# Chunk sums in two fp32r passes, masked scores written in place, and another order at both ends of an adaLN block

## The chip, the cores and the metric

The kernel runs on one core of a Trainium2 chip, as one program. The metric is the device time of one execution in microseconds. The baseline is the median of three runs.

## What is computed

One adaLN-modulated block on x of 8 batches x 256 tokens x 128 channels, all in float32. A vector c of each batch gives six modulation rows of 128. The first half is a Mamba-2 style mixer, the second is a small transformer layer with a mixture of experts. Cut to what matters:

```
sa, ca, ga, sb, cb, gb = silu(c) @ wmod                     # ga, gb: sign(.) * max(|.|, 0.25)
h = layernorm(x) * (1 + ca) + sa
x = x + ga * mixer(h)
h = layernorm(x) * (1 + cb) + sb
x = x + gb * layer(h)

mixer: A = -exp(A_log) * softplus(h @ W_dt)                 # 4 heads
       conv over 4 taps of 384 channels, PReLU -> X (4 heads x 64), B (64), C (64)
       L[l, s] = exp(sum of A over s+1..l)  for s <= l      # the chunk sums
       Y = (C B^T * L) X  + carried state;  out = layernorm(gelu(h W2) * Y) W3
layer: rmsnorm, 16 heads of 8 with rotary embedding, causal softmax, Wo, residual,
       rmsnorm, router over 8 experts, best 2, silu(x Wg) * (x Wu) Wd with hidden 384, residual
```

## The kernel before, in words

The work is a sequence of three blocks, each with one program for every engine and barriers between them. Engines are ordered by semaphores alone.

**First block (pre).** SyncE loads PACK0 (c and wmod), PACK1, the four taps of the convolution weights CW, and PACK2. TensorE computes the modulation columns (L510), then *folds* the input projection into each tap (`fold`, three fp32 matmuls of 384 columns in bank 5 or 6, evicted to VH by ScalarE and split to VL by VectorE). `turned` transposes four normalised tiles. `modulate(b)` computes the modulation rows of batch b by one fp32 matmul of 512 columns (L535) in the same two banks, evicted by ScalarE to MB. `group` makes the dt and gelu projections of two batches (L527). The order on TensorE is written out: fold 0, fold 1, then transposes, two modulates and a group in turn, then modulates 4 to 7, fold 2, two groups, fold 3.

**Main block.** Eight batches go through stages A (convolution), B (mixer), C (attention) and D (router). `ORDER` gives for each engine one list of steps; a step with `-k` works in round r on batch r - k. Each engine runs its list round after round, in that order. PSUM banks are shared by fixed lists, and a bank is written again when its reader's semaphore says so. The steps of interest:

- `a_g(t)` on GpSimd (L1526): the product of a triangle TRI and the decays DA of one chunk, 128 x 512, into G (named DAT in the profile).
- `b_seg(t)` on TensorE (L837): the chunk sums, one fp32 matmul of the triangle UP with G; ScalarE takes the exponential into EL (L1072), GpSimd multiplies EL by CBS (L1536).
- `c_s(n)` on VectorE (L1385): for each group of heads, scores plus causal mask, reduced by max into MX. The elementwise result goes to JUNK in SBUF and is read by nobody. The negated maxima MN (L1396) are transposed (L938), copied to MT and sent by DMA into QT, for the second computation of the scores (`c_p`, L959), whose exponential ScalarE writes to PT.
- `signed` on VectorE (L1476 to L1483, tiles SIGN and MAG) treats the gates of MB in the first rounds.
- GpSimd also takes roots (RSB, RSX, RSR, RMD), sends rows to the experts' buffer (L289), and clears the masked half of PT (L1582). On the last batch ScalarE rounds the expert weights to EARLY_H, and VectorE (L1498) and GpSimd (L1590) subtract for EARLY_L.

**Expert block (moe).** 39 blocks of 128 rows in chunks of four. ScalarE's queue loads WD. TensorE counts rows (L1890), waits for WD and for the table of experts, warms up with ten fp32 matmuls of 512 columns (L1947), transposes the first block (`turn`, L1904), and then for each block runs gate and up (L1919), transposes the product (L1930) and multiplies by WD (L1939). ScalarE and VectorE split the transposed rows into XH and XL (`halves`). SyncE loads XB, one block at a time (L1721), when the sends have landed. GpSimd scatters results to rows_by_token (L1743). When all have landed, SyncE loads four YL tiles; VectorE adds the two experts' rows (L1877), multiplies by the gate (L1880), adds x (L1883), for four groups in turn; SyncE stores each.

## Time and profile before

| | us |
|---|---|
| three timed runs, median (lowest to highest) | 476.73 (475.59 to 480.74) |
| the profiled execution | 474.64 |
| its span, first to last instruction | 472.9 |
| busy: TensorE, VectorE, ScalarE, GpSimd | 383.0, 313.7, 242.4, 215.1 |
| mean granted TensorE clock | 0.875 |

The profile is of one execution. Start times count from the span's first instruction. A matmul in fp32 appears as two passes, one in fp32r as one; the ends of matmuls are modelled, so a busy TensorE isn't one at its peak. A line number is that of the listing above.

### The profile page before, as it was taken

The page shows a single profiled execution, that of the slowest core. Times are in us where ns is not written, and L with a number is a line of the kernel's source. Part 1 is how long each engine was busy: PE and PEld are TensorE (multiplying, and loading weights), DVE is VectorE, ACT ScalarE, POOL GpSimd, SP SyncE. Part 2 cuts the span into 40 slices and gives each one's busy share as a digit, 9 for nine tenths or more (in the row PEclk, how much of TensorE's full clock was granted, in tenths as well). Part 3 has the DMA queues.
Part 4 walks back from the last instruction along what each step waited for, and adds up shares of the span by engine and source line. Part 5 has one row for each costly group of instructions (what it writes and reads, how often), then busy time and mean ns, then how long its engine had stood idle before and what let it go on. Part 6 is the DMA issues. An engine that isn't in the chain of part 4 may idle for free. (4 is left out here: it accounts for less than half of the span.)

```text
span 472.9 us, 9431 instructions
## 1 busy us (share of the span) xinstructions
PE 383.0 (81%) x2798; PEld 296.5 (63%) x2798; DVE 313.7 (66%) x1255; ACT 242.4 (51%) x600; POOL 215.1 (45%) x253
## 2 busy tenths in 40 slices
PE   1796898697999999999898887856528899999940
PEld 1455777474768777777575654634313799999930
DVE  3523499987979899998969576478250455545416
ACT  1175643472767858587664737755210445545510
POOL 1111335443454774757564352656430169644430
PEclk9998799997999999999968696755658999999985
DMA  8300000000201102030120552002041112212116
GB/s 300 122 0 2 0 1 0 3 0 2 94 1 37 60 25 94 15 104 14 34 74 23 199 186 93 20 6 95 23 154 47 29 49 61 73 49 59 34 56 236
DMA packets 20993, 29.24 MB, mean 62 GB/s; under 512 B 2322, under 2 KB 17816, under 8 KB 20560
## 3 DMA queue, kind: packets, MB, share of 16 engines
q1 hardware_dynamic: 18240, 21.59, 13.9%
q0 software_dynamic: 2272, 4.43, 2.8%
q10 hardware_dynamic: 432, 2.62, 1.6%
q8 instruction: 24, 0.39, 0.4%
q14 instruction: 25, 0.20, 0.1%
HBM read 14.38 MB, written 14.25 MB: 61 GB/s over the span
## 5 line engine op out<-in xcount | busy, mean ns | idle before, releaser
L1385 DVE CUSTOM_DVE_ANT_0 JUNK<-bank,PACK 128x128 f32<-128x128 f32 (+1 forms) x256 | 74.2, 352 | 14.5 <-PE bank L927 14.5
L1743 POOL DMA_INDIRECT rows_by_token<-YB,IDX x39 | 38.1, 977 | 54.5 <-DVE YB L1849 50.1
L1169 ACT ACTIVATE PT<-bank 128x512 f32<-128x512 f32 x96 | 51.6, 617 | 17.3 <-PE bank L959 17.3
L1582 POOL TENSOR_SCALAR_AFFINE_SELECT PT<-PT 128x512 f32<-128x512 f32 x64 | 41.8, 671 | 20.1 <-ACT PT L1169 19.6
L289 POOL DMA_INDIRECT rows_by_expert<-XR,POS x32 | 32.0, 1001 | 16.5 <-POOLq L565 8.4
L800 PE MATMUL bank<-HTH,VH 128*128 128x256 f32 x96 | 31.9, 333 | 3.9 <-issue 3.9
L1863 DVE TENSOR_TENSOR GU<-bank,SG 128x384 f32<-128x384 f32 x39 | 21.7, 557 | 18.5 <-ACT SG L1788 14.5
L927 PE MATMUL bank<-KT,QT 32*128 32x128 f32 (+1 forms) x256 | 28.9, 327 | 5.4 <-DVE MX L1385 3.0
L1939 PE MATMUL bank<-WD,GUT 128*128 x234 | 32.6, 276 | 0.6 <-DVE YB L1849 0.6
L1919 PE MATMUL bank<-EARLY_H,XH 128*128 x78 | 29.6, 380 | 2.7 <-DVE XL L1832 2.1
L927 PEld LDWEIGHTS bank<-KT,QT 32*128 32x128 f32 x256 | 19.6, 201 | 19.1 <-DVE MX L1385 12.0
L1788 ACT ACTIVATE SG<-bank 128x384 f32<-128x384 f32 x39 | 19.2, 492 | 24.2 <-PE bank L1919 23.3
L959 PE MATMUL bank<-QT,KT 32*128 32x256 f32 (+1 forms) x256 | 24.8, 355 | 6.7 <-DMA QT<-MT 5.5
L1939 PEld LDWEIGHTS bank<-WD,GUT 128*128 128x128 f32 x234 | 29.2, 192 | 1.0 <-issue 1.0
L1570 POOL TENSOR_TENSOR QS<-TA,QS 128x256 fp32r<-128x256 f32 x16 | 11.9, 763 | 39.0 <-ACT QS L1134 39.0
L1536 POOL TENSOR_TENSOR EL<-EL,CBS 128x512 f32<-128x512 f32 x16 | 20.6, 1286 | 18.0 <-ACT EL L1072 11.7
L800 PE MATMUL bank<-HTL,VH 128*128 128x256 f32 x96 | 28.5, 297 | 0.0
L800 PE MATMUL bank<-HTH,VL 128*128 128x256 f32 x96 | 28.4, 296 | 0.0
L959 PEld LDWEIGHTS bank<-QT,KT 32*128 32x128 f32 x256 | 19.1, 234 | 12.9 <-DMA QT<-MT 5.9
L1849 DVE TENSOR_SCALAR YB<-bank,XB 128x128 f32<-128x128 f32 x39 | 13.7, 351 | 19.3 <-PE bank L1939 19.1
L1919 PE MATMUL bank<-EARLY_L,XH 128*128 x78 | 26.2, 336 | 0.0
L1919 PE MATMUL bank<-EARLY_H,XL 128*128 x78 | 26.2, 336 | 0.0
(246 smaller groups left out, 1047.6 us busy)
## 6 DMA issues: line engine op xcount, KB each, us to landing
rows_by_expert<-EMPTY SPq DMA_DIRECT2D x8, 1040.0 KB, 5.5
XB<-rows_by_expert SPq DMA_DIRECT2D x39, 65.0 KB, 1.8
CW<-in_convw SPq DMA_DIRECT2D x4, 576.0 KB, 10.6
YL<-rows_by_token SPq DMA_DIRECT2D x4, 512.0 KB, 5.2
RAW<-in_wg SPq DMA_DIRECT2D x1, 1536.0 KB, 7.0
RAW<-in_wu SPq DMA_DIRECT2D x1, 1536.0 KB, 11.7
WD<-in_wd ACTq DMA_DIRECT2D x1, 1536.0 KB, 7.2
X<-in_x ACTq DMA_DIRECT2D x2, 512.0 KB, 7.1
```

Source lines behind the costliest of these rows:

```text
L289: nc.gpsimd.indirect_dma_start(out=xs, out_offset=bass.IndirectOffsetOnAxis(ap=POS[p][:, n:n + 1], axis=0), in_=XR[p][:, n // 2, n % 2, :] ...
L800: last = pe.matmul(BANK[f"conv{c}"][:, 0:L], w, ht[:, steps_of(b, 1), k:k + L].rearrange("p b l -> p (b l)"), start=(k + m == 0), stop=(k ...
L927: last = pe.matmul(BANK[f"s{n}"][:, i * w:(i + 1) * w], QT[p][rows, g, t * 128:(t + 1) * 128], KT[p][rows, g, 0:w], start=True, stop=True)
L959: last = pe.matmul(BANK[f"p{n}"][:, i * w:(i + 1) * w], KT[p][rows, g, k], QT[p][rows, g, q], start=True, stop=True)
L1169: nc.scalar.activation(to, of, ACT.Exp, scale=AD ** -0.5).then_inc(p_ev.sem, 1)
L1385: last = nc.vector.tensor_tensor_reduce(out=JUNK[:, n % 2, i * w:(i + 1) * w], in0=BANK[f"s{n}"][:, i * w:(i + 1) * w], in1=MASK[:, 256 - ...
L1536: nc.gpsimd.tensor_tensor(EL[t][:], EL[t][:], CBS[:, t, :].unsqueeze(1).to_broadcast([128, NH, 128]), ALU.mult).then_inc(m_done.sem, 1)
L1582: nc.gpsimd.affine_select(out=block, in_=block, compare_op=ALU.is_ge, fill=0.0, base=0, pattern=[[0, NG], [1, 128]], channel_multiplier=-1 ...
L1743: nc.gpsimd.indirect_dma_start(out=yt, out_offset=bass.IndirectOffsetOnAxis(ap=IDX[c % NX][:, j:j + 1], axis=0), in_=YB[i % NYB][:], in_of ...
L1863: nc.vector.tensor_tensor(GU[i % 2][:], P[4 + i % 2][:, 0:HID], SG[i % 2][:], ALU.mult).then_inc(gu_done, 1)
L1919: last = pe.matmul(P[bank + i % 2][:, 0:HID], x[c % 2][:, at], w[n][:, bass.ds(e, 1), :].rearrange("p e h -> p (e h)"), start=(m == 0), st ...
L1939: last = pe.matmul(P[7][:, 0:D], GUT[i % 2][:, h * 128:(h + 1) * 128], WD[:, bass.ds(e, 1), h, :].rearrange("p e d -> p (e d)"), start=(h ...
```

## The change

It has five parts. The chunk sums are no longer one fp32 matmul but two fp32r matmuls into the same bank: the decays DA are split into a rounded part DAH and a remainder DAL, GpSimd forms a product with TRI for each, and TensorE accumulates both with a rounded copy of UP. The score reductions write their elementwise result over the scores in the bank instead of to JUNK, and no longer wait on the step before last; SIGN lies in O. In the first block, modulates 0 to 3 come before fold 0, modulates 4 to 7 take the places between the transposes and the groups, and fold 3 comes ahead of the last two groups. In the expert block, the warm-up has 8 matmuls and no longer waits for WD or the table; WD is waited for ahead of each down (it takes effect at the first), and two blocks are transposed before the first gate. At the end, YL 0 and 2 are loaded by SyncE and YL 1 and 3 by ScalarE's queue, group 1 is combined on GpSimd, and the stores go in the order 0, 2, 1, 3.

```diff
@@ pre, scalar @@
+                    for b in range(4):
+                        modulate(b)
                     fold(0)
                     fold(1)
...
-                    modulate(0)
-                    modulate(1)
+                    modulate(4)
+                    modulate(5)
                     group(0, 0)
-                    modulate(2)
-                    modulate(3)
+                    modulate(6)
+                    modulate(7)
                     group(1, 1)
-                    for b in range(4, B):
-                        modulate(b)
                     fold(2)
+                    fold(3)
                     group(2, 0)
                     group(3, 1)
-                    fold(3)
@@ pre, tensor @@
-                    pe.wait_ge(mod_col, 2)
-                    pe.wait_ge(in_pack[1], DMA)
...
                     def modulate(b):
-                        if b < 2:
-                            pe.wait_ge(v_lo, b + 1)
-                        else:
+                        if b in (4, 5):
+                            pe.wait_ge(v_lo, b - 3)
+                        elif b >= 2:
                             pe.wait_ge(mb_ev, b - 1)
...
                     def fold(k):
                         pe.wait_ge(in_conv[k], DMA)
+                        pe.wait_ge(mb_ev, k + 3 if k < 2 else B)
                         if k >= 2:
-                            pe.wait_ge(mb_ev, B)
                             pe.wait_ge(v_lo, k - 1)
...
+                    for b in range(4):
+                        modulate(b)
+                    pe.wait_ge(mod_col, 2)
+                    pe.wait_ge(in_pack[1], DMA)
                     fold(0)
                     fold(1)
                     turned(0, 0)
                     for g in range(NGRP - 2):
                         turned(g + 1, (g + 1) % 2)
-                        modulate(2 * g)
-                        modulate(2 * g + 1)
+                        modulate(4 + 2 * g)
+                        modulate(4 + 2 * g + 1)
                         group(g, g % 2)
                     turned(NGRP - 1, 1)
-                    for b in range(4, B):
-                        modulate(b)
                     fold(2)
+                    fold(3)
                     group(NGRP - 2, 0)
                     group(NGRP - 1, 1)
-                    fold(3)
@@ main @@
-                G = [ms(f"DAT{t}", [128, NH, 128]) for t in range(T)]
+                GH = [ms(f"DATH{t}", [128, NH, 128], R) for t in range(T)]
+                GL = [ms(f"DATL{t}", [128, NH, 128], R) for t in range(T)]
+                DAH, DAL = ms("DAH", [128, B * T, NH], R), ms("DAL", [128, B * T, NH], R)
+                UP_R = ms("UP_R", [128, 128], R)
...
-                JUNK = ms("JUNK", [128, 2, 4 * 128])
...
-                SIGN, MAG = ms("SIGN", [128, 2, D]), ms("MAG", [128, 2, D])
+                SIGN, MAG = O[:].rearrange("p t h d -> p t (h d)"), ms("MAG", [128, 2, D])
...
-                            pe.matmul(BANK[f"seg{t}"][:], UP, G[t][:].rearrange("p h l -> p (h l)"),
-                                      start=True, stop=True).then_inc(seg_ps.sem, 1)
+                            pe.matmul(BANK[f"seg{t}"][:], UP_R[:], GH[t][:].rearrange("p h l -> p (h l)"),
+                                      start=True, stop=False)
+                            pe.matmul(BANK[f"seg{t}"][:], UP_R[:], GL[t][:].rearrange("p h l -> p (h l)"),
+                                      start=False, stop=True).then_inc(seg_ps.sem, 1)
...
-                            need(dve, s_max.sem, s_max.at(b, n - 1))
                             apart(dve, parted)
                             for i, g in enumerate(gs):
                                 last = nc.vector.tensor_tensor_reduce(
-                                    out=JUNK[:, n % 2, i * w:(i + 1) * w],
+                                    out=BANK[f"s{n}"][:, i * w:(i + 1) * w],
...
+                        need(dve, dt_fix, 10)
+                        nc.vector.tensor_copy(UP_R[:], UP)
+                        nc.vector.tensor_copy(DAH[:], DA[:]).then_inc(da_split, 1)
+                        need(dve, da_split, 1)
+                        nc.vector.tensor_tensor(DAL[:], DA[:], DAH[:].bitcast(F), ALU.subtract).then_inc(da_split, 1)
...
-                                need(pool, dt_fix, 10)
+                                need(pool, da_split, 2)
                             need(pool, seg_ps.sem, seg_ps.at(b - 1, t + 1))
...
+                            for to, of in ((GH, DAH), (GL, DAL)):
+                                last = nc.gpsimd.tensor_tensor(
+                                    to[t][:], TRI.unsqueeze(1).to_broadcast([128, NH, 128]),
+                                    of[:, steps_of(b * 2 + t, 1), :].bitcast(F).rearrange("p t h -> p (t h)")
+                                    .unsqueeze(2).to_broadcast([128, NH, 128]), ALU.mult)
+                            last.then_inc(g_done.sem, 1)
@@ moe @@
-            NX, NYB, WARM_UP = 3, 4, 10
+            POOLS = 1
+            NX, NYB, WARM_UP = 3, 4, 8
...
-                return P[1 if part[0] == 1 else 0][:, 0:128]
+                return P[part[0] % 2][:, 0:128]
...
-                for g in range(B // 2):
+                for g in (0, 2):
                     sp.dma_start(YL[g][:], by_token[:, 4 * g:4 * g + 4]).then_inc(yl_in[g], DMA)
-                for g in range(B // 2):
+                for g in (0, 2, 1, 3):
                     sp.wait_ge(fin[g], 3)
...
+                need(pool, yl_in[POOLS], DMA)
...
+                nc.gpsimd.tensor_tensor(RES[POOLS][:], YL[POOLS][:, :, 0, :], YL[POOLS][:, :, 1, :], ALU.add
+                                        ).then_inc(fin[POOLS], 1)
...
                 halves(0, 0)
+                halves(0, 1)
                 for i in range(NBLK):
-                    if 0 <= i < CHK - 1:
+                    if 1 <= i < CHK - 1:
                         halves(0, i + 1)
...
+                for k in range(NYB):
+                    need(act, y_out[k], DMA * len(range(k, NBLK, NYB)))
+                for g in (1, 3):
+                    act.dma_start(YL[g][:], by_token[:, 4 * g:4 * g + 4]).then_inc(yl_in[g], DMA)
...
-                        need(pe, x_lo, 2)
+                        need(pe, x_lo, upto(0))
...
-                        need(pe, x_lo, 1 if n == 2 else 3)
+                        need(pe, x_lo, n - 1)
...
                 def down(i, e):
+                    need(pe, in_wd, DMA)
...
-                need(pe, in_wd, DMA)
-                need(pe, tbl_exp, 1)
                 for i in range(WARM_UP):
                     pe.matmul(P[2 + i % 2][:], IDENT, PACK[0][:, 0:512], start=True, stop=True)
+                need(pe, tbl_exp, 1)
                 turn(0, 0)
+                turn(0, 1)
...
-                    if i < CHK - 1:
-                        turn(0, i + 1)
+                    if i < CHK - 2:
+                        turn(0, i + 2)
```

## Rows read from the trace of the kernel before

**Rows 1.** Table by stretch: busy us and instructions of each engine, granted clock, DMA.

```profile
120.00:240.00 120.00, 115.61 (x1034) 86.15 (x1034) 108.76 (x506) 85.28 (x224) 70.73 (x90) 0.98 0.16 54
347.70:366.60 18.90, 10.94 (x24) 4.95 (x24) 4.45 (x17) 1.85 (x3) 3.93 (x4) 0.73 0.39 126
```

**Rows 2.** Timeline of VectorE, two rounds: start, length, then idle before, releaser.

```profile
164.28 0.29 DVE L1385 CUSTOM_DVE_ANT_0 JUNK<-bank,PACK 128x128 f32<-128x128 f32 x1 [0.40 <-PE bank L927]
...
192.60 0.29 DVE L1385 CUSTOM_DVE_ANT_0 JUNK<-bank,PACK 128x128 f32<-128x128 f32 x1 [0.40 <-PE bank L927]
```

**Rows 3.** Timeline of the first stage.

```profile
11.15 6.86 PE L544 MATMUL bank<-CW,PACK 128*128 128x384 f32 x12 [3.86 <-DMA CW<-in_convw]
...
17.85 0.60 PE L520 MATMUL bank<-PACK,XN 128*128 128x128 f32 x4
...
29.42 3.69 PE L535 MATMUL bank<-PACK,SIL 128*128 128x512 f32 x8
...
35.86 3.68 PE L527 MATMUL bank<-PACK,HG 128*128 128x260 f32 x16
...
39.38 2.10 PE L544 MATMUL bank<-CW,PACK 128*128 128x384 f32 x6
...
42.04 0.56 DVE L453 TENSOR_TENSOR VL<-bank,VH 128x384 fp32r<-128x384 f32 x1 [4.90 <-ACT VH L411]
```

**Rows 4.** Timeline of TensorE around a chunk sum; one row of the chain.

```profile
168.30 1.02 PE L837 MATMUL bank<-DAT,PACK 128*128 128x512 f32 x2
169.25 0.50 PE L927 MATMUL bank<-KT,QT 32*128 32x256 f32 x4
...
374.31 1.04 PE bank L1919 x6
```

**Rows 5.** GpSimd's products as a group; VectorE in the timeline.

```profile
L1526 POOL TENSOR_TENSOR DAT<-PACK,DA 128x512 f32<-128x512 f32 x16 | 17.3, 1082 | 15.2 <-DVE DA L1451 9.4 <-PE bank L837 5.6
...
74.89 1.50 DVE L1477 SCALAR_TENSOR_TENSOR MAG<-MB 128x256 f32<-128x256 f32 x1
...
65.05 0.42 DVE L1477 SCALAR_TENSOR_TENSOR MAG<-MB 128x256 f32<-128x256 f32 x1
...
173.91 0.88 DVE L187 TENSOR_SCALAR VED<-SSD 128x2 f32<-128x2 f32 x1
```

**Rows 6.** Groups of VectorE by form: busy us, mean ns, idle before, releaser.

```profile
L1385 DVE CUSTOM_DVE_ANT_0 JUNK<-bank,PACK 128x256 f32<-128x256 f32 x128 | 47.0, 419 | 4.9 <-PE bank L927 4.9
L1385 DVE CUSTOM_DVE_ANT_0 JUNK<-bank,PACK 128x128 f32<-128x128 f32 x128 | 27.7, 285 | 9.5 <-PE bank L927 9.5
...
L1303 DVE TENSOR_TENSOR GO<-bank,MB 128x256 f32<-128x256 f32 x8 | 3.3, 417 | 1.2 <-PE bank L879 1.1
L1359 DVE TENSOR_TENSOR TB<-QK,PACK 128x256 f32<-128x256 f32 x8 | 3.3, 417 | 0.0
```

**Rows 7.** Start of the experts: timeline, DMA issues, chain.

```profile
355.19 10.25 PE L1947 MATMUL bank<-PACK 128*128 128x512 f32 x20 [6.62 <-DMA WD<-in_wd]
356.79 13.02 SPq L1721 DMA_DIRECT2D XB<-rows_by_expert  x12
...
XB<-rows_by_expert SPq DMA_DIRECT2D x39, 65.0 KB, 1.8
...
373.20 0.44 PE bank L1904 x4
```

**Rows 8.** Tail and two streams at once: chain, timeline, a group.

```profile
458.22 3.84 DMA YL<-rows_by_token
...
462.15 0.69 DVE L1877 TENSOR_TENSOR RES<-YL 128x512 f32<-128x512 f32 x1 [7.09 <-DMA YL<-rows_by_token]
...
L1752 POOL TENSOR_TENSOR H<-H,MB 128x512 f32<-128x512 f32 x4 | 5.2, 1309 | 0.1
...
325.86 6.44 DVE L1498 TENSOR_TENSOR EARLY_L<-RAW,EARLY_H 128x384 fp32r<-128x384 f32 x8
325.87 3.75 POOL L1582 TENSOR_SCALAR_AFFINE_SELECT PT<-PT 128x512 f32<-128x512 f32 x4 [0.23 <-ACT PT L1169]
```

More of the change, by code:

```diff
@@ L1475, in signed @@
                             need(dve, mod_fix, n + 3 * i)
-                            nc.vector.tensor_scalar(SIGN[:], MB[:, now, m, :], 0.0, 2.0, ALU.is_ge, ALU.mult)
+                            nc.vector.tensor_scalar(SIGN, MB[:, now, m, :], 0.0, 2.0, ALU.is_ge, ALU.mult)
                             nc.vector.scalar_tensor_tensor(out=MAG[:], in0=MB[:, now, m, :], scalar=-1.0,
@@ L1482, in signed @@
                             need(dve, mod_fix, n + 3 * i + 2)
-                            nc.vector.scalar_tensor_tensor(out=MB[:, now, m, :], in0=SIGN[:], scalar=-1.0,
+                            nc.vector.scalar_tensor_tensor(out=MB[:, now, m, :], in0=SIGN, scalar=-1.0,
                                                            in1=MAG[:], op0=ALU.add, op1=ALU.mult
@@ L1758, in _ @@
                                                     ).then_inc(base, 1)
+                need(pool, yl_in[POOLS], DMA)
+                by_batch = RES[POOLS][:].rearrange("p (b t) d -> p b t d", t=T)
+                nc.gpsimd.tensor_tensor(RES[POOLS][:], YL[POOLS][:, :, 0, :], YL[POOLS][:, :, 1, :], ALU.add
+                                        ).then_inc(fin[POOLS], 1)
+                need(pool, fin[POOLS], 1)
+                nc.gpsimd.tensor_tensor(by_batch, by_batch, MB[:, steps_of(POOLS * 2, 2), GB, :].unsqueeze(2)
+                                        .to_broadcast([128, 2, T, D]), ALU.mult).then_inc(fin[POOLS], 1)
+                need(pool, fin[POOLS], 2)
+                nc.gpsimd.tensor_tensor(RES[POOLS][:], RES[POOLS][:], X[:, steps_of(POOLS * 4, 4), :], ALU.add
+                                        ).then_inc(fin[POOLS], 1)
             @block.scalar
@@ L1873, in _, with combined @@
                 need(dve, base, B)
[L1874 to L1884 removed]
+                def combined(g, n):
+                    by_batch = RES[g][:].rearrange("p (b t) d -> p b t d", t=T)
+                    if n == 0:
+                        need(dve, yl_in[g], DMA)
+                        nc.vector.tensor_tensor(RES[g][:], YL[g][:, :, 0, :], YL[g][:, :, 1, :], ALU.add
+                                                ).then_inc(fin[g], 1)
+                    elif n == 1:
+                        need(dve, fin[g], 1)
+                        nc.vector.tensor_tensor(by_batch, by_batch, MB[:, steps_of(g * 2, 2), GB, :].unsqueeze(2)
+                                                .to_broadcast([128, 2, T, D]), ALU.mult).then_inc(fin[g], 1)
+                    else:
+                        need(dve, fin[g], 2)
+                        nc.vector.tensor_tensor(RES[g][:], RES[g][:], X[:, steps_of(g * 4, 4), :], ALU.add
+                                                ).then_inc(fin[g], 1)
+                for g in range(B // 2):
+                    for n in range(3 if g != POOLS else 0):
+                        combined(g, n)
             @block.tensor
```

16 lines of the change are left out of this document (2 added, 14 removed).

## The prediction

> **What bounds the kernel now.** I read the page first, then the table by stage, then the two ends and one round of the middle in order of time. The page names TensorE and VectorE as the busiest, but the table by stage shows that no engine bounds all of it. I use five stages: the first (0 to 42.6 us), the main one (to 347.7), the start of the experts (to 366.6), the expert blocks (to 455) and the tail (to 472.9). In the middle of the main stage, 120 to 240 us, TensorE is busy 115.61 of 120 us and VectorE 108.76 [rows 1]: two engines run nearly full and hand a short wait to and fro. At the first scores of a round VectorE waits 0.40 us for TensorE, at 164.28 and again one round of 28.3 us later [rows 2]. That wait is what TensorE can give back in such a round; what it saves beyond that is not seen. At the start of the experts TensorE is busy 10.94 of 18.90 us [rows 1], most of it warm-up. The expert blocks are one unbroken chain of TensorE.
>
> The profiled execution took 474.64 us for a span of 472.9; the three timed runs have the median 476.73 (475.59 to 480.74). I sum against 474.64 and add 1.0 at the end, about half of what the profiled run lies under the median.
>
> **First stage.** It is a chain on TensorE [rows 3]. TensorE idles 3.86 us until the first CW has landed at 11.15, folds twice (L544), transposes from 17.85, and later runs eight modulate passes (L535) from 29.42. A fold follows, two groups (L527) from 35.86 for 3.68 us, the last fold from 39.38 for 2.10 us, and that fold's split on VectorE ends at 42.60, 1.1 us behind it. The change puts four modulates into the idle time before 11.15 (their operands come with the first pack), and the last fold ahead of the two groups. So from 29.42 there remain two folds and the groups: 29.4 + 2 x 2.1 + 3.7 = 37.3, and with 1.0 us for the evictions behind the last group 38.3 against 42.6: **-4.3 us**. The new waits of the folds ask for modulates' evictions that are finished by then. The first folds run at the low clock now, as their row shows: 12 passes in 6.86 us, where the last fold does 6 in 2.10 [rows 3]. TensorE begins its steady work some 3.8 us earlier after the change, and if the clock rises as long after that as now, the folds themselves run at the full rate and end up to 1.8 us before 17.85; if it doesn't, four modulates at the low rate (1.7 us each, from the eight passes in 3.69 at the full one) push the folds back and they end where they do now. I take the middle, **-0.8**. Together -5.1, ends -4 and -6.5.
>
> **Chunk sums.** Each sum was one fp32 matmul of 512 columns, two passes in the records, 0.95 us from its start at 168.30 to the next at 169.25 [rows 4], twice that at the half clock. The new pair of fp32r passes has no row of 512 columns. The nearest is L1919: six passes of 384 columns in 1.04 us [rows 4], 0.173 each, so 0.23 for 512 and 0.46 a pair. Sixteen sums save 16 x 0.49 = 7.8 us of TensorE, up to 9 with those at the half clock. Little of it lies on the path: in a steady round the first sum stands ahead of VectorE's wait of 0.40 us, the second ahead of VectorE work that is late anyway. Six such waits and 1 us for a sum at the half clock near 112 us give -3.4. Ends: 0 if VectorE's wait has another cause, -9 if all counts.
>
> GpSimd pays for it. Each operand was one product of 1.08 us, 17.3 us in 16 [rows 5]; now there are two, so +17 us. GpSimd is half idle and almost nobody waits for it, so the product as such is hidden. But a VectorE instruction that reads two SBUF operands, or a TENSOR_SCALAR in SBUF, stands still while a GpSimd instruction runs: MAG takes 1.50 us at 74.89 and 0.42 at 65.05, and VED, of two elements, 0.88 us at 173.91, beside a product [rows 5]. The score reductions read one operand from PSUM; with means of 419 and 285 ns they are not touched, and their 74.7 us in eight batches are a third of a round [rows 6]. So of 17 us two thirds meet VectorE work that can be stopped, and such work waits for half a product on average: 17 x 0.67 x 0.5 = **+5.6** (0 to +11, if each waits for all of it). Behind a round's second product GpSimd has RMD, RSR and an EL product, which come 1.05 us later, and ScalarE's XR and QK after them; in the two rounds where scatters fill GpSimd's queue that can cost 1 us more, which the upper end holds. The set-up adds three short VectorE instructions and a wait of GpSimd's first product on them (0.6 us); TensorE's first sum waits for a table load of ScalarE anyway, so nothing. Main stage: -3.4 + 5.6 = **+2.2**, ends -7 and +9.
>
> **Scores in place.** VectorE's 256 reductions write into the bank that they read and no longer to JUNK. Their own wait on the step before last goes; VectorE is idle ahead of them for TensorE alone (4.9 and 9.5 us, all for L927, [rows 6]), so it was free. No row here has VectorE write to PSUM. Lower bound: nothing, since reading from PSUM costs nothing either (GO from PSUM 417 ns, TB from SBUF 417 ns, both of 256 columns, [rows 6]). Upper bound: read and write of one bank exclude each other and each element counts twice; 128 more columns are 134 ns, so 128 x 0.134 + 128 x 0.268 = 51 us. I take 0, because the equal pair is nearest. Where JUNK and SIGN lie moves no instruction.
>
> The Trainium skill (VectorE: DVE Perf Modes, section on the TRN2 errata) gives a VectorE instruction 58 cycles of fixed cost from SBUF and 120 from PSUM. The equal pair above does not show that difference. Were the 62 cycles (65 ns at its 0.96 GHz) to come with a write to PSUM, the estimate would be 256 x 65 ns = 17 us of VectorE.
>
> **Start of the experts.** TensorE waits 6.62 us for WD, warms up for 10.25 us from 355.19 and only then turns the first block [rows 7]. The change warms up at once, with 8, and waits for WD only at the first down; WD lands at 355.2 and then has nothing behind it. Warming up from 348.6 takes 8.2 us at today's mean, 13.7 if all of it runs at the half clock; the end is 357 (362). Next in line is the load of the blocks: SyncE issues 12 of them in 13.02 us from 356.79, 1.085 apart, each landing 1.8 us later [rows 7], the first at 358.6. The first expert matmul then comes near 360.1. But the transposes of the second chunk need the eighth block: issue 364.4, landing 366.2 or a little later. They stand at 373.20 in the chain now [rows 7], and behind them all is as before and full. Gain: 373.2 - 366.6 = 6.6 us. TensorE idles some 2.5 us ahead of that landing, and a stretch of half clock behind it would cost 1.5 to 3. I take **-5.2** (-2.5 to -6.6).
>
> **Tail.** One queue loads four YL; the first lands 3.84 us after its issue, and VectorE runs 12 instructions of 0.69 us, 8.3 us in all [rows 8]. After the change YL0 and YL1 are issued side by side and share the DMA, so YL0 lands later. VectorE keeps nine, GpSimd takes three, of 1.3 us by the nearest row, L1752 of the same shape [rows 8]. Both read two SBUF operands. What two such streams cost together is seen at 325.86: eight VectorE subtractions of 384 columns take 6.44 us, 0.8 each and twice what their length asks, while four GpSimd selects take 3.75 [rows 8]: they take turns. So 9 x 0.69 + 3 x 1.3 = 10.1 us against 8.3, less 0.6 for overlap, is +1.2, and the later landing +0.6: **+1.8** (-1 to +3). The Trainium skill (SBUF — State Buffer, section Who interferes with whom) calls the pair of ports that the two engines share an exclusive lock; by that rule, the turns of 325.86 agree.
>
> Sum: -5.1 + 2.2 + 0 - 5.2 + 1.8 = -6.3; 474.64 - 6.3 + 1.0 = **469.3 us**, 1.6% under the median. A measurement of this kernel can tell about 1% from no change.
>
> **The rivals.** (a) Contention eats the gain, no change: the added products stop VectorE for most of their length (+10), the sums give -3.4, the tail +3, the ends -4.5 and -4.5. That is +0.6, **476 us**. For it: VED waited almost a whole product. Against: many products fall beside the reductions. (b) TensorE sets the rounds, and all it saves counts: -9 + 3 there, -6 and -6 at the ends, tail 0: -18, **458 us**. Against it stands VectorE with 108.76 us busy in 120. (c) Slower: the write into the bank just read lengthens each reduction. Some 160 of the 256 stand before 240 us, where VectorE has no slack, so the gain of 6.3 is gone from 6.3/160 = 39 ns an instruction on; at the upper bound of 51 us some 35 are exposed, **504 us**, at half of it 487. For it speaks only that no row shows such a write. (d) The reordering at the start of the experts buys nothing because the clock falls back: start -2.5, inside my range.
>
> **Chances.** Forecast (464.5 to 472) 0.53; (a), 472 to 478, 0.25; (b), 457 to 464.5, 0.12; (c), 478 and above, 0.10. The range, 462 to 477, leaves out (c) and the far parts of (a) and (b). Faster by over 1% is under 472.0: 0.53 + 0.12 = 0.65; (a) is the middle, 0.25; (c) is slower, 0.10.
>
> **What would show it.** The first stage ends near 38. The sums are two fp32r passes, 0.46 us a pair; GpSimd has 32 products; HN, MAG, MB, VED and VER grow in mean, and VectorE's busy time up to 240 us rises by 5 us. The reductions stay at 285 and 419 ns; if they grow, (c) is on. The first expert matmul comes 12.5 us after the stage begins, with a wait for XB ahead of the second chunk's transposes. In the tail VectorE's RES instructions grow from 0.69 to some 1.5 us while GpSimd's run. The prediction fails if a round of the main stage changes by more than 1 us either way.

## The result and the profile after

The changed kernel takes 489.54 us (489.43 to 492.46, three runs) against 476.73: the ratio is 1.027, 95% interval 1.0185 to 1.0355. It is slower, by 12.8 us where 7.4 less were forecast. The profiled execution has a span of 487.7 us against 472.9. Executions of one kernel here can lie 10 us apart and more, each with its own mean clock, so a small difference of two medians says little.

I put the same instruction of both traces side by side at the borders of the stages. The first stage ends 4.28 us earlier than before; the main stage is 23.1 us longer (its end stands 18.83 later); the start of the experts takes back 5.72; the expert blocks are equal; the tail costs 1.7. That is -4.3 + 23.1 - 5.7 + 1.7 = 14.8, the whole difference. So three of the four stages that were changed do what was forecast, and the loss is in the middle.

Table by stretch of the kernel after, columns as in [rows 1]: the steady part of the main stage, then a look at 170 to 190 us in steps of 4.

```profile
120.00:240.00 120.00, 112.59 (x970) 86.48 (x970) 102.46 (x455) 78.46 (x198) 70.25 (x89) 0.90 0.13 44
...
174.00:178.00 4.00, 4.00 (x29) 3.23 (x30) 3.97 (x13) 2.66 (x12) 3.59 (x4) 1.00 0.10 33
178.00:182.00 4.00, 2.46 (x16) 1.69 (x15) 3.93 (x17) 3.15 (x10) 2.08 (x3) 0.94 0.00 0
182.00:186.00 4.00, 4.00 (x15) 3.23 (x16) 3.68 (x16) 2.04 (x6) 1.32 (x2) 0.50 0.69 229
186.00:190.00 4.00, 4.00 (x22) 3.55 (x21) 1.27 (x3) 1.71 (x4) 0.09 (x1) 0.50 0.14 48
```

The granted clock from 120 to 240 us is 0.90 where it was 0.98 [rows 1]. TensorE is busy 2.46 of 4 us from 178, and behind that it works at the lower of its two levels, 1.2 GHz, for some 10 us (181.5 to 191.8 in a table by single microseconds). The kernel before has no such stretch there: its rows of 120 to 230 us are all at 1.00.

What VectorE does before that, in the groups by form (all of VectorE, to compare with [rows 6]) and in the timeline from 165 and from 175 us:

```profile
L1389 DVE CUSTOM_DVE_ANT_0 bank<-bank,PACK 128x256 f32<-128x256 f32 x128 | 50.8, 453 | 1.9 <-PE bank L932 1.8
L1389 DVE DVE_READ_ACCUMULATOR2_ANT MX<- 128x1 f32 x256 | 35.5, 139 | 0.0
L1389 DVE CUSTOM_DVE_ANT_0 bank<-bank,PACK 128x128 f32<-128x128 f32 x128 | 32.3, 326 | 14.1 <-PE bank L932 14.0
```

```profile
165.42 0.33 DVE L1389 CUSTOM_DVE_ANT_0 bank<-bank,PACK 128x128 f32<-128x128 f32 x1
165.67 0.14 DVE L1389 DVE_READ_ACCUMULATOR2_ANT MX<- 128x1 f32 x1
165.67 0.33 DVE L1389 CUSTOM_DVE_ANT_0 bank<-bank,PACK 128x128 f32<-128x128 f32 x1
...
175.26 1.06 POOL L1537 TENSOR_TENSOR DATH<-PACK,DAH 128x512 fp32r<-128x512 f32 x1
175.46 1.88 DVE L187 TENSOR_SCALAR VED<-SSD 128x2 f32<-128x2 f32 x1
176.25 1.05 POOL L1537 TENSOR_TENSOR DATL<-PACK,DAL 128x512 fp32r<-128x512 f32 x1
```

Two things are seen. The reductions grew from 285 to 326 and from 419 to 453 ns, and reading the accumulator from 82 to 139. They overlap, so the price is read from start to start: the median over 128 each is 0.249 us against 0.211 for 128 columns and 0.382 against 0.345 for 256. That is 38 ns for either length, a fixed cost. And VED, two elements long, took 1.88 us: it waited for both products, one after the other, where it took 0.88 beside one [rows 5]. This happens in two of the eight rounds, as before; in the other six VED takes 0.16 to 0.17 us.

The edges, in the timeline of the kernel after. The last two folds run as one block, and the groups end at 37.5; the warm-up starts by itself and the first expert matmul stands 13.35 us after the stage's begin; a sum is two passes.

```profile
29.95 4.04 PE L542 MATMUL bank<-CW,PACK 128*128 128x384 f32 x12
...
33.83 3.68 PE L525 MATMUL bank<-PACK,HG 128*128 128x260 f32 x16
...
377.86 0.30 PE L1942 MATMUL bank<-PACK,XB 128*128 128x128 f32 x1 [0.81 <-DMA XB<-rows_by_expert]
...
379.85 0.68 PE L1957 MATMUL bank<-EARLY_H,XH 128*128 x1 [0.73 <-ACT XH L1796]
```

```profile
476.08 0.69 DVE L1909 TENSOR_TENSOR RES<-YL 128x512 f32<-128x512 f32 x1 [7.91 <-DMA YL<-rows_by_token]
476.52 1.37 POOL L1775 TENSOR_TENSOR RES<-YL 128x512 f32<-128x512 f32 x1 [6.61 <-DMA YL<-rows_by_token]
476.81 1.63 DVE L1913 TENSOR_TENSOR RES<-RES,MB 128x512 f32<-128x512 f32 x1
...
484.59 0.69 DVE L1917 TENSOR_TENSOR RES<-RES,X 128x512 f32<-128x512 f32 x1
```

In the tail VectorE's instructions grow to 1.63 us while GpSimd's run, and the combine takes 9.2 us instead of 8.3.

### The profile page after: what moved, and what is told of

Read it like the earlier page. It is cut to its first block and busy times, and to the rows that moved or that the text cites. A ratio compares the mean times of both kernels' runs of the same rounds, so it can differ in the third digit from the quotient of the medians.

```text
span 487.7 us, 9446 instructions
## 1 busy us (share of the span) xinstructions
PE 399.6 (82%) x2794; PEld 314.0 (64%) x2794; DVE 329.3 (68%) x1255; ACT 244.0 (50%) x600; POOL 236.7 (49%) x272
## 5 line engine op out<-in xcount | busy, mean ns | idle before, releaser
L1389 DVE CUSTOM_DVE_ANT_0 bank<-bank,PACK 128x128 f32<-128x128 f32 (+1 forms) x256 | 82.5, 390 | 15.9 <-PE bank L932 15.8
L289 POOL DMA_INDIRECT rows_by_expert<-XR,POS x32 | 31.8, 993 | 16.5 <-POOLq L565 8.4
L1893 DVE TENSOR_TENSOR GU<-bank,SG 128x384 f32<-128x384 f32 x39 | 21.7, 557 | 22.2 <-ACT SG L1813 14.0
L932 PE MATMUL bank<-KT,QT 32*128 32x128 f32 (+1 forms) x256 | 29.7, 336 | 7.9 <-DVE MX L1389 4.3
L1389 DVE DVE_READ_ACCUMULATOR2_ANT MX<- 128x1 f32 x256 | 35.5, 139 | 0.0
L803 PE MATMUL bank<-HTH,VH 128*128 128x256 f32 x96 | 32.2, 335 | 3.7 <-issue 3.7
L1582 POOL TENSOR_TENSOR QS<-TA,QS 128x256 fp32r<-128x256 f32 x16 | 11.9, 764 | 41.1 <-ACT QS L1139 41.1
L964 PE MATMUL bank<-QT,KT 32*128 32x256 f32 (+1 forms) x256 | 26.3, 371 | 5.7 <-DMA QT<-MT 4.6
L803 PE MATMUL bank<-HTH,VL 128*128 128x256 f32 x96 | 30.3, 316 | 0.0
L803 PE MATMUL bank<-HTL,VH 128*128 128x256 f32 x96 | 30.2, 314 | 0.0
L1978 PEld LDWEIGHTS bank<-WD,GUT 128*128 128x128 f32 x234 | 29.2, 192 | 1.0 <-issue 1.0
L964 PEld LDWEIGHTS bank<-QT,KT 32*128 32x128 f32 x256 | 20.5, 249 | 10.6 <-DMA QT<-MT 4.8
L981 PE MATMUL bank<-PT,V 128*32 128x256 f32 x256 | 26.0, 475 | 1.6 <-POOL PT L1594 1.4
## 6 DMA issues: line engine op xcount, KB each, us to landing
RAW<-in_wu SPq DMA_DIRECT2D x1, 1536.0 KB, 11.9
```

Of the source, the lines that this page charges most:

```text
L289: nc.gpsimd.indirect_dma_start(out=xs, out_offset=bass.IndirectOffsetOnAxis(ap=POS[p][:, n:n + 1], axis=0), in_=XR[p][:, n // 2, n % 2, :] ...
L803: last = pe.matmul(BANK[f"conv{c}"][:, 0:L], w, ht[:, steps_of(b, 1), k:k + L].rearrange("p b l -> p (b l)"), start=(k + m == 0), stop=(k ...
L932: last = pe.matmul(BANK[f"s{n}"][:, i * w:(i + 1) * w], QT[p][rows, g, t * 128:(t + 1) * 128], KT[p][rows, g, 0:w], start=True, stop=True)
L964: last = pe.matmul(BANK[f"p{n}"][:, i * w:(i + 1) * w], KT[p][rows, g, k], QT[p][rows, g, q], start=True, stop=True)
L981: pe.matmul(o[:, at:at + L], V9[p][:, 0, h, :], PT[:, j, g, 0:L], start=True, stop=False, tile_position=(0, 32 * g))
L1389: last = nc.vector.tensor_tensor_reduce(out=BANK[f"s{n}"][:, i * w:(i + 1) * w], in0=BANK[f"s{n}"][:, i * w:(i + 1) * w], in1=MASK[:, 256 ...
```

## The experiments

Each is compared with the kernel before on the same chip. Medians are given with the lowest and highest time and, where there is one, the ratio with its 95% interval; the mechanism is read from the one profiled execution. Five chips were used (e1 to e4, e5 to e8, e9 to e12, e13 to e15, e16 and e17), on which the kernel before had medians of 476.1 to 479.7, so microseconds of different groups compare less well than ratios. All but e4 and e12 start from e1 or from e3.

| run | what it is | us, median (lowest to highest) | ratio to before |
|---|---|---|---|
| e1 | ends only | 467.88 (467.2 to 468.9) | 0.9835 (0.980 to 0.987) |
| e2 | + in place | 479.56 (473.5 to 481.6) | 1.003 (0.999 to 1.008) |
| e3 | + split sums | 476.80 (473.1 to 483.3) | 0.999 (0.994 to 1.003) |
| e4 | after, old tail | 488.73 (486.5 to 490.8) | 1.027 (1.021 to 1.032) |
| e5 | + second product alone | 483.03 (481.5 to 487.6) | 1.012 (1.003 to 1.021) |
| e6 | + fp32r sums, one product | 465.70 (462.7 to 480.3) | 0.9685 (0.961 to 0.976) |
| e7 | + 1.4 us of VectorE once | 470.26 (469.3 to 474.2) | 0.985 (0.977 to 0.993) |
| e8 | e3, VED and VER on GpSimd | 470.20 (469.9 to 470.4) | 0.982 (0.976 to 0.988) |
| e9 | e1, VED and VER on GpSimd | 475.36 (470.4 to 485.1) | 0.998 (0.992 to 1.004) |
| e10 | e9, old tail | 482.17 (471.4 to 487.4) | 1.0225 (1.011 to 1.034) |
| e11 | e3, product moved | 493.05 (487.8 to 495.3) | 1.043 (1.034 to 1.053) |
| e12 | after, VED and VER on GpSimd | 484.82 (483.3 to 489.5) | 1.023 (1.018 to 1.029) |
| e13 | e1, EL waits for MN | 471.82 (465.0 to 479.9) | none |
| e14 | e9, EL waits for MN | 474.01 (469.2 to 475.5) | 0.995 (0.991 to 1.000) |
| e15 | e11, product waits for MN | 475.96 (470.4 to 480.1) | none |
| e16 | e1 again | 469.23 (468.0 to 474.6) | 0.986 (0.980 to 0.992) |
| e17 | e1, old tail | 467.17 (465.2 to 474.1) | 0.978 (0.973 to 0.984) |

Where rounds are spoken of, this is the distance between the first BATCH_NORM_STATS2 on STATB of one batch and the next, for batches 0 to 7, in us:

| kernel | rounds |
|---|---|
| before | 17.7 15.8 25.8 29.1 28.3 27.9 27.7 |
| after | 18.7 18.8 26.1 29.8 34.2 31.4 29.8 |
| e1 | 17.7 17.0 26.2 29.1 28.3 27.9 27.3 |
| e2 | 17.7 17.1 26.4 29.8 29.0 29.2 31.0 |
| e3 | 18.7 18.6 25.8 28.9 32.1 31.2 28.1 |
| e7 | 17.7 16.7 27.0 29.1 32.7 27.7 26.6 |
| e8 | 18.7 18.6 25.7 28.6 28.5 29.1 28.7 |
| e9 | 17.6 17.0 26.1 29.2 31.8 28.3 27.7 |
| e10 | 17.6 16.8 27.0 29.1 28.9 29.7 30.1 |
| e11 | 18.7 17.8 27.5 33.2 34.5 32.4 29.4 |
| e12 | 18.7 18.6 26.0 29.5 32.5 32.2 30.4 |
| e15 | 18.7 18.0 27.7 29.8 28.5 28.5 27.5 |

**e1, e2, e3: the parts.** e1 undoes both edits of the main stage, with the wait on s_max and the one fp32 matmul; e2 and e3 undo one each:

```
-                                    out=BANK[f"s{n}"][:, i * w:(i + 1) * w],
+                                    out=JUNK[:, n % 2, i * w:(i + 1) * w],
...
-                            for to, of in ((GH, DAH), (GL, DAL)):
...
+                            nc.gpsimd.tensor_tensor(
+                                G[t][:], TRI.unsqueeze(1).to_broadcast([128, NH, 128]),
```

> The kernel after with its two edits of the main stage undone: the reductions write to JUNK again, and a chunk sum is one fp32 matmul over one GpSimd product. Left of the change: first stage, start of the experts, tail. Theory A (the loss comes from the two edits of the main stage, the rest works as predicted): the span shows -4.3 us at the end of the first stage, the main stage is as long as before (305 us within 3), the start of the experts gives -6, the tail +1.7, so 464 to 467 us. Theory B (the clock did it: the first stage starts the rounds at another phase of the clock, and the rounds lose by that alone): the main stage is 10 us or more longer than before though its instructions are the same, and the time is 476 or more.

> e1 and the reductions writing in place, into the bank that they read. The sums stay one fp32 matmul over one product. Theory A1 (the write to PSUM is the main cost): each reduction keeps the 38 ns more from start to start that the kernel after shows (0.249 against 0.211 us for 128 columns, 0.382 against 0.345 for 256), 256 of them 9.7 us of VectorE, most of it exposed and with more half clock behind it: 475 to 485 us. Theory A2 (GpSimd's second product is the main cost): 38 ns a reduction stay, but in the rounds where TensorE has slack or the clock is low they hide, at most 4 us over e1: under 471.

> e1 and the split chunk sums: two fp32r passes over two GpSimd products. The reductions write to JUNK as in the kernel before; for want of space JUNK is of two bytes an element here and shares its space with MAG. The start-to-start time of a reduction should be 0.211 and 0.345 us whatever the type; if it is not, the type of the output counts and the run says less. Theory A2 (GpSimd's second product holds VectorE up, VED above all, which took 1.88 us at 175.46 against 0.88 before, and TensorE then idles and loses its clock): VED stays near 1.9 us in these rounds and the time is 8 us or more over e1, 474 or more. Theory A1: sums save 0.49 us each and the products cost as much, within 3 us of e1: 463 to 469.

Theory A holds and B is out: e1's steady rounds are those of the kernel before to 0.1 us, and it is 1.65% faster than before (467.88 us, 0.9 over the range that I gave). In place alone costs 11.7 us over e1, the split alone 8.9, and both together (the kernel after) 21.7: nearly their sum. A1 and A2 were put as alternatives; both are true. In the profiled executions the main stage grows by 1.8 us in e1, 12.0 in e2, 11.9 in e3 and 23.1 in the kernel after. For the spread of one execution: e16, which has e1's instructions, shows 4.8 where e1 shows 1.8. e2 keeps the 38 ns (medians 0.249 and 0.382); e3 has 0.211 and 0.345 with its two-byte JUNK.

```profile
171.88 2.27 DVE L187 TENSOR_SCALAR VED<-SSD 128x2 f32<-128x2 f32 x1
172.08 1.05 POOL L1540 TENSOR_TENSOR DATH<-PACK,DAH 128x512 fp32r<-128x512 f32 x1
173.08 1.04 POOL L1540 TENSOR_TENSOR DATL<-PACK,DAL 128x512 fp32r<-128x512 f32 x1
```

```profile
174.00:178.00 4.00, 2.30 (x14) 1.32 (x12) 3.93 (x19) 2.41 (x8) 2.77 (x4) 1.00 0.00 0
...
182.00:186.00 4.00, 4.00 (x22) 3.55 (x21) 1.78 (x5) 2.07 (x4) 1.39 (x3) 0.50 0.34 113
```

These are e3's timeline and its table by stretch: VED stands until the second product ends, TensorE runs dry, and the clock falls. Nothing in e3's reductions changed but the type of JUNK.

What TensorE waited for from 120 to 240 us (total, times, longest), in e1 and then in e3:

```profile
PE bank L938 <- DVE MN L1399: 0.9, 2, 0.5
```

```profile
PE bank L945 <- DVE MN L1406: 2.1, 4, 0.7
PE bank L208 <- ACT XR L202: 2.1, 2, 1.0
```

So the late VED reaches TensorE on two ways. One is VectorE's own order: MN comes later. The other is longer: GpSimd takes the root RMD of VED, ScalarE makes XR with it, and TensorE's L208 needs XR. Of the 1.7 us that TensorE idles from 174 to 178 us, 1.00 is for XR and 0.70 for MN; in e1 it never waits for XR in these rounds.

**e4: the tail undone in the kernel after** (one queue, twelve instructions on VectorE).

> The kernel after with the tail undone: four loads of YL on SyncE's queue, all twelve instructions of the combine on VectorE, stores in order. All else as after. By the trace of after the tail grew by 1.7 us (from the last expert block to the end: 22.8 to 24.6 us), of it 1.0 while VectorE's instructions take 1.6 us beside GpSimd's. If that is the cause: 1.5 to 2 us less than the kernel after, 487.5 us, and each RES instruction at 0.69 us. If the later landing on two queues is nothing but a shift of the same bytes: less than 0.7.

0.8 us less, inside the spread and under the 1.5 to 2 expected; in the trace the tail is 1.8 us shorter, and each RES takes 0.69 us.

**e5, e6: the product and the sums apart.** e5 makes the one product of e1 twice (the added lines above the mark in the middle), e6 takes e3 and reads the high half twice, without the low product:

```
+                            for sem in (once, g_done.sem):
...
+                                if sem is once:
+                                    need(pool, once, 2 * b + t + 1)
...
-                            pe.matmul(BANK[f"seg{t}"][:], UP_R[:], GL[t][:].rearrange("p h l -> p (h l)"),
+                            pe.matmul(BANK[f"seg{t}"][:], UP_R[:], GH[t][:].rearrange("p h l -> p (h l)"),
```

> e1 (ends of the change alone, 467.88 us) with each GpSimd product made twice, the sums still one fp32 matmul: the added product without what it is for. Theory C (the loss of e3 is the product: two in a row hold VectorE's two-element VED for up to 2.3 us, TensorE runs out of work at the end of the round and its clock is halved): the time is 9 to 14 us over e1, 477 to 482, above e3's 476.8 by what the fp32r passes save; VED takes 1.9 us or more in the rounds from 171 and 202. Theory D (the loss of e3 comes from the fp32r sums themselves, say a TensorE with less work that loses its clock): within 2 us of e1.

> e3 with one product: both fp32r passes read the high half (the low half's product is left out, so the low part of each decay is missing from the sums and the high part counts twice). The saved TensorE time without GpSimd's second product. Theory C: the sums save 0.5 us each and nothing is held up longer than before, 1 to 4 us under e1, 464 to 467. Theory D: 4 us or more over e1, 472 or more.

The product alone costs 2.9% (1.012 against e1's 0.9835; 15 us by the medians). The sums alone gain 2.2 us by the medians and 1.5%, some 7 us, by the ratios, since the kernel before was slower beside e6 than beside e1 (479.7 against 477.8); between these it stays open. D is out. e6's profiled execution is its slowest (480.3, the other four 462.7 to 467.2), so no row of it is used. A point I had wrong is seen in e5:

```profile
175.73 0.88 DVE L187 TENSOR_SCALAR VED<-SSD 128x2 f32<-128x2 f32 x1
...
177.21 0.51 DVE L1347 TENSOR_SCALAR VER<-SS 128x2 f32<-128x2 f32 x1
...
179.01 1.26 POOL L1540 TENSOR_TENSOR EL<-EL,CBS 128x512 f32<-128x512 f32 x1
179.11 1.20 DVE L1397 TENSOR_SCALAR MN<-MX 128x32 fp32r<-128x32 f32 x1
```

Between its two products GpSimd waits on a semaphore, and VED slips in after one, 0.88 us, not the 1.9 expected. The loss is there all the same: everything behind the products on GpSimd is a microsecond late, so the EL product now starts just ahead of MN and holds it for all of its length. TensorE waits 0.6 us for XR and 0.6 for MN there.

**e7: one late VectorE step.**

```
+                        d_variance(dve, b)
+                        if b == 1:
+                            nc.vector.tensor_reduce(MAG[:, 0, 0:5], MASK[:].unsqueeze(1).to_broadcast([128, 5, 256]),
```

> e1 with one added VectorE instruction in one single round, behind VED of the second batch (at 169.5): the maximum of 5 x 256 columns of the mask, some 1.4 us, as long as VED was held more in e3 (2.27 against 0.88). Nothing else is changed and GpSimd does nothing more. Theory E (one late VectorE step of this size empties TensorE at the end of the round, and the chip then grants half the clock for some us): VectorE's next rounds stand 3 to 5 us later than in e1, with a stretch at half clock near 178 to 190 that e1 does not have; the whole run is 3 to 6 us over e1, if rounds further on lose by it too up to 9. Theory F (delays just add): 1.4 us, and TensorE's clock is as in e1 there.

```profile
171.21 1.48 DVE L1507 TENSOR_REDUCE MAG<-PACK 128x5 f32<-128x1280 f32 x1
```

```profile
174.00:178.00 4.00, 2.23 (x21) 2.22 (x21) 3.90 (x14) 2.97 (x8) 1.46 (x2) 1.00 0.01 4
178.00:182.00 4.00, 4.00 (x22) 3.20 (x20) 3.79 (x17) 1.42 (x5) 1.41 (x2) 0.58 0.81 270
182.00:186.00 4.00, 4.00 (x30) 3.75 (x30) 0.53 (x4) 2.78 (x6) 1.22 (x2) 0.56 0.01 2
```

Theory E for the round: one instruction that VectorE is 1.4 us later by makes that round 4.3 us longer (32.7 against 28.3), with half clock from 178.6 on. For the whole run it was too high: in the trace two thirds are given back later, where half clock falls in other places, and the median is 2.4 us over e1 and 1.0 over e16, which has e1's instructions. So a growth of the round is shown, and a loss of the whole run is not.

**e8, e9, e10, e12: VED and VER on GpSimd**, where their roots are taken (VER in the same way):

```
-            nc.vector.tensor_scalar(VED[:], SSD[:], 1.0 / D, RMS_EPS, ALU.mult, ALU.add
+            nc.gpsimd.tensor_scalar(VED[:], SSD[:], 1.0 / D, RMS_EPS, ALU.mult, ALU.add
```

> e3 (split sums, JUNK) with VED and VER computed by GpSimd, right ahead of the roots that take them, and no longer by VectorE. The two products stand where they stood. Theory C: no VectorE instruction of the round's end is held by the products, the clock stays up in 125 to 230 us as in e1, and the time is within 3 us of e1: 465 to 471. If the held VED is not the cause but GpSimd's later roots are (RMD and RSR come 1 us later than in e1, and ScalarE's XR and QK after them): the rounds stay as long as in e3, 474 to 479.

> e1 with VED and VER computed by GpSimd, as in e8, and one product a sum. In e1 VED waits 0.7 us for the product in two of the eight rounds, and the first MN 0.4 us for the EL product behind it. Theory C: VectorE gets these back in the rounds at full clock, but GpSimd's roots come 0.3 to 0.6 us later and QK behind them: 0 to 3 us under e1, 465 to 468. If the later roots cost more than the holds: over 469.

> e9 with the tail of the kernel before (one queue for the YL loads, the combine on VectorE alone). By e4 against the kernel after the change of the tail costs 0.8 us: 0.5 to 1.7 us under e9. If under 464, the fastest version so far.

> The kernel after with nothing else changed than VED and VER on GpSimd. In it both costs of the main stage act: the 38 ns more a reduction and the products. If the two costs are separate, this takes back what e8 took from e3 (6.6 us, from 489.5 to 481 to 485) and leaves e2's cost. If the reductions alone keep VectorE so late that TensorE loses its clock in any case: above 486.

e8 takes back 6.6 of e3's 8.9 us by the medians, and all of them by the ratios (0.982 against e1's 0.9835), with both products in place, and e3's two long rounds are gone (28.5 and 29.1). TensorE still waits 1.2 us for XR in such a round, but no longer for MN, and the clock from 172 to 202 us stays at 1.00. Its first two rounds are still 2.6 us longer than e1's together; by which instruction was not traced. e12 takes back 4.7 by the medians, inside the range expected of two separate costs, but this is weak: the ratios are 1.023 and 1.027 with intervals that overlap, and its profiled execution, the slowest, has long rounds (32.5 and 32.2) and a main stage as long as that of the kernel after (23.0 us over before). But e9, the same patch with one product, is a miss, 7.5 us over e1 by the medians, and 4.9 if in each kernel only the executions within 1.5% of its fastest are taken:

```profile
172.08 1.26 POOL L1530 TENSOR_TENSOR EL<-EL,CBS 128x512 f32<-128x512 f32 x1
172.23 1.15 DVE L1390 TENSOR_SCALAR MN<-MX 128x32 fp32r<-128x32 f32 x1
```

```profile
170.00:174.00 4.00, 3.00 (x19) 1.89 (x18) 3.21 (x12) 3.20 (x9) 3.03 (x5) 1.00 0.00 0
...
178.00:182.00 4.00, 4.00 (x22) 3.55 (x21) 2.18 (x5) 1.91 (x4) 1.41 (x3) 0.50 0.44 149
```

With VED gone VectorE comes to MN earlier and GpSimd to EL later, and MN is held 1.15 us, not 0.62 as in e1. MN is what TensorE waits for, 1.00 us here. e8 escapes it, for its EL starts after MN. Whether this is what e9 loses by is open. e10 has the same main stage, the same hold (1.16 us at 173.94) and the same wait of 1.00 us, and its clock stays at 1.00 from 122 to 202 us: that round takes 28.9 us, where e9's takes 31.8. And the traced execution of e9 is its fastest, with a main stage 4.8 us over before, as in e16. e10 is a miss as well: 0.5 to 1.7 us under e9 were expected, and its median is 6.8 over it, with executions 16 us apart; in its trace the tail alone is 1.8 us shorter, as it should be.

**e11, and the waits of e13 to e15.** e11 moves "Ag1" in GpSimd's order from ahead of RMD, RSR and EL to behind them. e13 to e15 add one wait, `need(pool, mn.sem, mn.at(..., 2))`, ahead of the second EL (e13, e14) or of the moved products (e15).

> e3 (split sums, JUNK) with the second chunk's two products moved in GpSimd's order from ahead of RMD, RSR and EL to behind them, where GpSimd waits 4.5 us for ScalarE. VED and VER stay on VectorE. Theory C: VED takes 0.2 to 0.4 us in all rounds; the products meet MN, XC and TA instead, which read SBUF twice or are held as VED was, and cost part of it back. 467 to 474. If it is not who is held but that there is a product at all (its traffic), the time stays as e3's, 475 to 478.

> e1 with one added wait: GpSimd's second EL product starts only when VectorE has written MN. In e1 the first MN takes 0.62 us at 172.50 beside that product, and TensorE waits 0.45 for it. Theory G (what counts is whether the step that TensorE waits for is held): MN 0.18 us in the rounds at full clock, TensorE's waits for MN go from 0.9 us to under 0.2 between 120 and 240 us, XC and TA are held instead without harm: 0 to 3 us under e1, 465 to 468. Theory H (the amount of contention counts, wherever it falls): no gain, 467 to 471.

> e9 (475.4; VED and VER on GpSimd) with the same added wait. Theory G: the first MN falls from 1.15 us to 0.18, TensorE's clock stays up from 125 to 215 us, and the time is 464 to 469, 6 us or more under e9. Theory H, or the later roots as the cause: as e9, 472 to 478.

> e11 (493.1; split sums, the second chunk's products behind EL) with the products waiting for MN. Theory G: both MN take 0.2 us instead of 0.9, TensorE's waits for MN go from 6.2 us to under 1.5 between 120 and 240, the rounds from 34 to 28.5 to 30, and the time is 467 to 476, 17 us or more under e11. Theory H: XC, TA and TB are held for the same 2 us, and the time stays over 485.

e11 is the slowest of all, though VED took 0.16 us. TensorE's waits from 120 to 240 us (total, times, longest) in e11 name the cause; in e15, under it, MN is down to 0.3 us, and these are the longest:

```profile
PE bank L945 <- DVE MN L1406: 6.2, 4, 1.7
```

```profile
PE bank L966 <- DVE HV L1259: 2.5, 4, 0.7
PE bank L895 <- DVE HX L1348: 1.0, 1, 1.0
...
PE bank L945 <- DVE MN L1406: 0.3, 1, 0.3
```

One wait, with the same instructions, brings e11 from 493.1 to 476.0 and its rounds from 34.5 to 28.5; the executions don't overlap (487.8 to 495.3, 470.4 to 480.1). That is theory G, and H, that contention costs the same wherever it falls, is out there. It mends what the move in e11 broke: against e3, 476.8 us, nothing is gained. And e13 and e14 say how far G goes; both came out where H had them, or above. Their MN are at 0.18 us and their steady clock up to 210 us is 1.00, and they gained nothing that can be told (e14 is 1.4 us under e9 by the medians, e13's executions span 15 us): XC and TA are held instead, and in e13 TensorE waits for PRIOR (0.7 us once) and POSB (0.5 once), which e1 does not show. So one more wait is worth it where TensorE stalls for 1.6 us a time (e11, 6.2 us in four waits); where it stalls for 0.5 (e1) or 1.0 (e9) no gain can be told.

**e16, e17: the best kernel.**

> The kernel of e1 once more, in five rounds: first stage, start of the experts and tail of the change, main stage as before. If e1 stands: 466 to 470 us, 0.98 to 0.985 of the kernel before, its interval clear of 1.

> e1 with the tail of the kernel before: one queue for the YL loads, twelve instructions of the combine on VectorE. The main stage has the same instructions in the same order. By the traces the combine takes 9.2 us in e1's form and 8.3 in this: 0.5 to 1.5 us under e16. If the new tail gains: 0.5 or more over e16.

e1 stands at 0.986, and with the old tail it is 0.978 (0.973 to 0.984), 2.1 us less than e16: the fastest version that computes everything, 467.2 us. The intervals of the two overlap; that the new tail costs is shown by the traces, where its length is much the same in every kernel that has it, 1.5 to 1.8 us over before (2.9 in e7), and 0.1 to 0.2 under before where the old one stands.

## Why the prediction was wrong

- **First stage**, -5.1 forecast: -4.28 in the kernel after, -5.2 in e1, e3 and e17, -5.7 in e16, -4.1 in e15. Right. (Four modulates at the low rate would be 1.84 us each by the eight passes in 3.69, not 1.7; nothing rested on it, for the first folds run at the full rate, 12 passes in 4.10 us.)
- **Start of the experts**, -5.2: -5.72, and -4.2 to -6.1 in all runs. Right, with waits for XB ahead of the first transposes (0.81 and 0.63 us) and of the second chunk's (0.29).
- **Tail**, +1.8: +1.7, with the turns that [rows 8] had shown. Right, though one reading was not: 0.8 us for 384 columns isn't twice what the length asks, for a VectorE instruction of 384 columns takes 0.557 us elsewhere in the same trace (GU).
- **Chunk sums on TensorE**: a pair was put at 0.46 us by L1919; from the first pass to the next instruction it is 0.66 us at the full clock, where the fp32 matmul in the same place took 1.05, so that sum saves 0.39 us, not 0.49. The round's other sum saves 0.07 (0.95 to 0.88), for the scores behind it then wait 0.17 for VectorE's O. A small error; e6, with the sums alone 2 to 7 us under e1, fits the 3.4 us that I gave them in all.
- **GpSimd's product**, +5.6: the step that failed first. "Such work waits for half a product on average" is a mean over instructions that are not alike. As VectorE's time the mean was near: its busy time in the main stage is 247.2 us in e5 against 241.0 in e1, 6.2 more. As time of the kernel it was not. A hold lasts as long as GpSimd has products back to back (2.27 us for VED), and what it costs depends on who waits. VED had its row among those I read, with its product beside it. Two chains start at it, and I followed neither to TensorE: VED and MN, and VED, RMD and XR, which I named with QK and put at 1 us, in two rounds, in the upper end alone. Measured: 10 us for product and sums together (e3's main stage against e1's, 11.9 against 1.8), some 14 for the product alone (e5).
- **Scores in place**, 0: mis-sized. I took the read as the nearest row for a write. It is 38 ns an instruction, 9.7 us of VectorE, and rival (c) had set the point from which it decides at 39 ns. In the whole it costs 11.7 us, more than its own length. Whether it comes with any write to PSUM or only with a write into the bank being read stays open: no run writes into another bank.
- **The term that was missing** is the clock in the middle. My sum had the clock at both ends only; in the main stage I let delays add. e7 shows that in a round they don't: 1.4 us late at the round's end is 4.3 us of that round. For the whole main stage the tables by single microseconds show what the 23.1 us consist of. TensorE idles 53.6 us in it, before 45.6: 8.0 more. It is busy at half clock for 116 us, before 71, and each of these microseconds does half the work: 22 more. The work itself is 7 us less, counted at the full rate; this comes with the fp32r sums (e3 and e8 show it, e2 doesn't). So the largest part is the clock. In e2 it is nearly all: 94 us busy at half clock against 76 in e1, 9.4 of its 10.2 us. A part of this is chance: e16, with e1's instructions, has 87 (5.9 us). This is bookkeeping and not a cause: it doesn't say which delay made which stretch. By its own sign the prediction failed too, for four rounds changed by 2.1 to 5.9 us, where 1 was the limit.

Of the rivals, (c) named the sign and the place, but the mechanism is only half of it; (a) had the other half and the wrong price. That (c) also had the time, 487 at half its bound, is luck: half its bound is 100 ns an instruction, and 38 were measured; by its own rule that is no gain and no loss, and in place alone (e2) is at 1.003. The page VectorE: DVE Perf Modes (section on the TRN2 errata) of the Trainium skill would give 65 ns, an estimate by the 62 cycles between its two fixed costs, if they came with a write to PSUM; a fixed price is there, and the measurement is 38. By the Trainium skill (SBUF — State Buffer, section Who interferes with whom) the shared ports are locked exclusively for the whole of an instruction; VED's 0.88 us beside one product agrees, and that it waited 2.27 us, through a second one as well, is what these traces add.

## What to carry to other kernels

Price contention by the instruction that is held and by who waits for it, never by a mean: one wait that moved a product off the wrong instruction was worth 17 us (e11 to e15), though the order that needed it was no better than the one it came from. When TensorE is nearly full, a delay at the point where it waits can cost itself and the clock behind it, so look at the idle time that an edit adds there, not at busy sums. An output that nobody reads still has a price that depends on where it goes: 38 ns more in PSUM than in SBUF here. And trace one kernel more than once before explaining a difference of a few microseconds: e1 and e16, the same instructions, are 3.0 us apart in the main stage alone.

## What the runs showed of the hardware

A tensor_tensor_reduce that writes its bank instead of SBUF costs 38 ns more from start to start, for 128 and for 256 columns alike, and its accumulator read 139 ns instead of 82. A TENSOR_SCALAR of two elements in SBUF waited 2.27 us for two GpSimd products back to back, and 0.88 when a semaphore wait stood between them. TensorE at the full clock idled 1.7 us from 174 to 178 us (e3) or 1.8 (e7) and was then granted half the clock for some 7 us of work (some 10 in the kernel after, behind 1.5 us idle); in e1, with 0.45 us idle in the same place, it kept it. Between these the length of the idle time alone did not decide: one wait of 1.00 us was followed by some 7 us of half clock in e9 and by none in e10, which has the same main stage, and one of 1.24 us by none in e8.
